# Four transposes per expert, spread over the inner blocks of a mixture-of-experts stage

## The reference

```python
h = jnp.square(jax.nn.relu(jnp.einsum('ecd,edf->ecf', expert_in, w_key)))
expert_out = jnp.einsum('ecf,efd->ecd', h, w_value)
```

## Time and profile before

| what | value |
|---|---|
| runs of the kernel before | 4043.54, 4044.42 and 4046.9 us, median 4044.42 us |
| profiled execution, own time | 4040.18 us |
| its span, first to last instruction | 4038.5 us |
| PE busy in the span | 3852.3 us |
| DVE busy in the span | 3071.3 us |
| ACT busy in the span | 1747.6 us |
| mean granted TensorE clock | 0.989 of 2.4 GHz |

### The profile page before, as it was taken

One profiled execution on the slowest core, in us unless ns is written; L12 is line 12 of the kernel. 1 busy time (PEld: TensorE's weight loads), 2 busy tenths in 40 slices (PEclk: granted clock), 3 DMA queues, 4 the chain that ended last, 5 costly groups with the idle time before them and its releaser, 6 DMA issues. The chain is left out here.

```text
span 4038.5 us, 112515 instructions
## 1 busy us (share of the span) xinstructions
PE 3852.3 (95%) x44162; PEld 2550.8 (63%) x44162; DVE 3071.3 (76%) x9981; ACT 1747.6 (43%) x5452; POOL 297.4 (7%) x345
## 2 busy tenths in 40 slices
PE   7999999999999999999999999999879999999996
PEld 5566666666656666665666666666547777778543
DVE  8788888888878888887888888875555555555598
ACT  5344444443444444433444444444334444444465
POOL 2000000000000000000000000000000000000353
PEclk9999999999999999999999999999989999999998
DMA  5411111112111111121111111110134455545674
GB/s 212 120 28 28 28 36 28 33 30 38 28 28 28 35 28 28 33 39 30 28 28 28 35 28 33 31 27 12 59 99 169 170 185 189 176 166 190 216 263 154
DMA packets 421707, 317.36 MB, mean 79 GB/s; under 512 B 298217, under 2 KB 331497, under 8 KB 418132
## 3 DMA queue, kind: packets, MB, share of 16 engines
q1 hardware_dynamic: 399488, 234.57, 22.4%
q0 software_dynamic: 17696, 66.79, 4.2%
q10 hardware_dynamic: 4020, 9.10, 0.6%
HBM read 210.03 MB, written 100.70 MB: 77 GB/s over the span
## 5 line engine op out<-in xcount | busy, mean ns | idle before, releaser
L470 PE MATMUL bank<-buf,buf 128*16 128x256 f32 x32768 | 1873.0, 380 | 76.1 <-DVE buf L854 64.0
L470 PEld LDWEIGHTS bank<-buf,buf 128*16 128x16 f32 x32768 | 905.9, 97 | 885.6 <-DVE buf L854 98.7
L993 PE MATMUL bank<-buf,buf 128*128 128x256 f32 (+1 forms) x3072 | 1039.3, 338 | 2.7 <-DVE buf L1309 1.5
L994 PE MATMUL bank<-buf,buf 128*128 128x256 f32 (+1 forms) x3072 | 980.6, 319 | 0.0
L995 PE MATMUL bank<-buf,buf 128*128 128x256 f32 (+1 forms) x3072 | 980.4, 319 | 0.0
L731 DVE SCALAR_TENSOR_TENSOR buf<-buf,buf,buf 128x256 f32<-128x256 f32 x1860 | 846.6, 481 | 1.6 <-issue 1.6
L832 DVE STREAM_TRANSPOSE buf<-bank 128x256 f32<-128x256 f32 x1024 | 458.4, 448 | 398.8 <-PE bank L470 351.7
L683 ACT ACTIVATE buf<-buf 128x96 f32<-128x96 f32 x1024 | 290.5, 284 | 1061.1 <-DVE buf L837 1060.5
L993 PEld LDWEIGHTS bank<-buf,buf 128*128 128x128 f32 x3072 | 581.0, 189 | 255.6 <-issue 211.7
L995 PEld LDWEIGHTS bank<-buf,buf 128*128 128x128 f32 x3072 | 582.9, 190 | 44.3
L994 PEld LDWEIGHTS bank<-buf,buf 128*128 128x128 f32 x3072 | 583.7, 190 | 41.3
(11 more groups left out here) (155 smaller groups left out, 2980.9 us busy)
## 6 DMA issues: line engine op xcount, KB each, us to landing
buf<-in_wk SPq DMA_DIRECT2D x16, 2048.0 KB, 10.8
buf<-in_wv SPq DMA_DIRECT2D x16, 2048.0 KB, 9.3
buf<-x_scratch SPq DMA_DIRECT2D x32, 1024.0 KB, 7.7
buf<-in_xT SPq DMA_DIRECT2D x62, 496.0 KB, 3.9
buf<-in_xB SPq DMA_DIRECT2D x32, 512.0 KB, 3.7
expert_in_scratch<-buf POOLq DMA_DIRECT2D x16, 1024.0 KB, 23.8
x_scratch<-buf SPq DMA_DIRECT2D x32, 512.0 KB, 9.6
buf<-expert_in_scratch SPq DMA_DIRECT2D x16, 1024.0 KB, 12.5
```

Of the source, the lines that this page charges most:

```text
L470: last = mm(gate_ps[hf][32 * j:32 * j + B, 0:HCOLS], hist[:, k, at_step(slot_at)], wh[:, k, j * GCOLS + hf * HCOLS:j * GCOLS + (hf + 1) * ...
L993: nc.tensor.matmul(out, left[0], right[0], start=first, stop=False)
L994: nc.tensor.matmul(out, left[0], right[1], start=False, stop=False)
```

## The change

The four turns of the next expert's rows, k = 0, 1, 2 and 3, stood behind the inner blocks 3, 4, 5 and 6. They now stand behind the blocks 1, 3, 5 and 7. On DVE the splits stood behind the work of the hidden blocks 4, 5, 6 and 7; they now stand behind that of 2, 4, 6 and, for the last, behind the loop over the blocks, which is again behind block 7.

```diff
-    TURN_FROM = 3
+    TURN_AT = (1, 3, 5, 7)
...
-                    if f >= TURN_FROM and f < TURN_FROM + KD and not is_last(e):
-                        turn(e + 1, 1 - par, f - TURN_FROM)
+                    if f in TURN_AT and not is_last(e):
+                        turn(e + 1, 1 - par, TURN_AT.index(f))
...
-                    if f > TURN_FROM and f <= TURN_FROM + KD and not is_last(e):
-                        split_x(e + 1, 1 - par, f - TURN_FROM - 1)
+                    if f - 1 in TURN_AT and not is_last(e):
+                        split_x(e + 1, 1 - par, TURN_AT.index(f - 1))
                 if not is_last(e):
+                    split_x(e + 1, 1 - par, KD - 1)
                     first.low_wk(dve, e + 1)
```

## The result

The changed kernel takes 4021.3 us (median of four runs, 4020.51 to 4023.53); the kernel before, timed beside it, 4045.66 us (4043.54 to 4046.97). The ratio is 0.9943 with a 95% interval of 0.9928 to 0.9958: 24.4 us faster, between 17 and 29 by the interval. The profiled execution took 4020.97 us, with a span of 4019.2 us.

The account below looks back on a forecast made before the run. PE was taken to bound the expert phase, its pauses for DVE included. 22.2 us gained less 1.5 us of pace gave -20.7 us, set on the 4044.42 us median: 4023.7 us, range 4018 to 4030.

Parts of the forecast that it names:

- The pause: PE's wait at turn 2 for DVE's split of turn 0, experts 0 to 14: gone, 22.2 us gained.
- The pace behind a turn: Inner blocks behind the first turn: 24 matmuls per expert may start slower, 1.5 us lost over 15 experts.
- The seam, DVE and the queues: Turn 3 between block 7 and the first product, moved splits, load order: no cost, zero us.
- The margins ahead of turns 2 and 3: Time between the end of the split each turn waits for and its start: some 4.5 and 5 us.
- The sum: Whole kernel: 22.2 us gained less 1.5 us of pace, -20.7 us; chance of the forecast 0.89.
- the wait stays: Turn 2's pause is not DVE's doing and remains: nothing gained, 4045.9 us; chance 0.03.
- part comes back at the seam: Turn 3 between block 7 and the products costs 6.8 us more: gain 13.9 us, 4030.5 us; chance 0.06.
- the clock falls between the turns: Blocks 2 and 3: 24 matmuls per expert at 1.2 GHz cost 72 us, 4096 us; chance 0.02.
- the rule of the Trainium skill weighed against the change: Matmuls should run back to back, as power scales with use; cutting 48 to 24 ahead of the first turn speaks against it.

Follow-up runs that it names:

- the last experiment: Against the kernel before, PE's order kept but every split on DVE moved one hidden block later (behind blocks 5, 6, 7 and the loop); 4218.8 us in one run.

## Why the prediction was right

**The pause.** Forecast 22.2 us, 1.48 per expert. The experiment that left PE's order alone gained 47.54 - 46.045 = 1.495 per expert, 22.4 us: the term, refilling included, not the 19.3 us of idle time alone. Its cause is shown twice, by moving the split and by adding a bank.

**The pace behind a turn.** This is the term of the sum that failed: "24 matmuls per expert may run at the slower pace", 1.5 us charged. In the timeline after, six distances behind the first turn take 3321.65 - 3320.26 = 1.39 us, 0.232 each, and the 16 from there to the end of block 3 take 3325.27 - 3321.65 = 3.62, 0.226 each. Behind turn 1 the tail is longer: ten distances take 3328.49 - 3326.17 = 2.32 us, 0.232 each, and the 12 after them 3331.21 - 3328.49 = 2.72, 0.227 each. The slowness is a short tail of six to ten matmuls behind each turn, not a state that lasts from the first turn on. The rows of before did not tell these apart as I used them, since a turn stood behind every block from 3 to 6 and I averaged over a whole block. Four tails stood in inner blocks before and three stand there after, for the products run at their own 0.2324 anyway; so the term is not a loss of 1.5 but a gain of 0.03 to 0.04 us per expert, half a us, which is the difference that the experiment with turn 3 behind block 6 shows. That the tail is where it comes from is worked out from these distances, not tested by itself.

**The seam, DVE and the queues.** Forecast nothing, and nothing was found: no wait at the first products, the margin there 1.8 us where 1.6 and something more for turn 3 were forecast, expert 0's earlier first turn without a pause. The margins ahead of turns 2 and 3 were put at 4.5 and 5 us and are 4.1 each. The prediction took PE's way there from the old order, but turns have left it: between block 2 and turn 2 PE now makes one turn less, and between block 4 and turn 3 two less, at nearly half a us each.

**The sum.** Forecast -20.7, from 22.2 gained and 1.5 lost; by the periods -23.0, and by the phase of the profiled executions -23.4. The medians give -24.4, with an interval that holds all three. The time, 4021.3, lies 2.4 us under the forecast 4023.7.

**The rivals.** That the wait stays is refuted by the list of waits. That part comes back at the seam is refuted by the timeline and by the experiment that takes turn 3 away from it. That the clock falls between the turns did not happen: 1.00 from 3000 to 3740 us.

This last rival had less for it than the prediction says. Its batch of 48 matmuls ahead of the first turn was counted from block 0, but PE goes straight on from one expert's products to the next expert's blocks: from turn 3 to the next turn 0 it was 12 + 96 + 48 = 156 matmuls and is 96 + 24 = 120 now, while between the other turns it was 12 and is 24. Batches of 12 had thus left the clock at 1.00 already. Nor did the low level of expert 0 begin in this phase, behind the wait for its rows. In the profile of before the clock is 0.50 ahead of that wait, which begins at 2968.0 us (2980.60 less 12.57):

```profile
2965.00:2968.00 3.00, 1.05 (x4) 0.71 (x4) 1.26 (x4) 1.31 (x4) 0.00 (x0) 0.50 0.45 52
```

```profile
2980.60 1.94 PE L1219 MATMUL bank<-buf,buf 128*128 128x128 f32 x8 [12.57 <-PEq L230]
```

By the rule of the Trainium skill weighed against the change (Perfetto Trace Analysis, Matmul Optimizations) batches cut short could have lowered the clock; the measurement decides against that for a batch of 24 matmuls between turns. For pauses of 4.46 us the last experiment agrees with the rule.

## What to carry to other kernels

When the engine that bounds a stage shows the same small pause once per round, find the instruction that ends it and ask where that instruction stands in its own engine's queue: here a producer with two banks waited for a consumer that stood one block of other work too late, and moving the consumer's work ahead, or a third bank, was worth the same. Price such a pause by the distance between starts, not by the idle time alone (1.48 us against 1.28), and price a small change on the stage it touches, since an untouched phase can differ by 3 us between two executions. When a slower pace is seen behind an event, look how far behind it lasts before charging it to everything that follows.

## What the runs showed of the hardware that was not expected

- A group of four transposes of 128 x 128 costs PE about 0.48 us among inner blocks, 0.35 of it until the next matmul starts and the rest in a slower first matmul (0.32 us to the next start) and a tail of six to ten that start 0.232 instead of 0.227 us apart. Between product groups it costs 0.43 to 0.46 us, by whichever pace of the products, 0.2336 or 0.2324 us, is taken. Why the products are slower, and why the tail ends, no run here tells.
- A pause of PE of 1.28 us once per expert left the granted clock at 1.00 in the kernel before. In one run, two pauses of 4.46 us per expert brought it to its lower level, 1.2 GHz, behind each of them, for 1.5 us and more of extra time per pause; PE had been busy without a gap ahead of the first.
